# Rotary attention: the band mask is added by a matmul with the identity instead of by a VectorE addition

## The chip, the cores and the metric

The kernel runs on one core of one Trainium2 chip. The metric is device time in microseconds (us) of one execution. The kernel computes a chain of twelve transformer-like blocks; the change touches one of them, the second, and this document follows that block.

## The reference, cut to what matters

```python
x = x + _L0_attn_ref(_layernorm(x, axis=-1), Wq, Wk, Wv, Wo)   # x is (128, 32, 128)

def _L0_attn_ref(x, Wq, Wk, Wv, Wo):          # 16 query heads, 4 key/value heads of width 8
    xq = _rope((x @ Wq).reshape(b, s, HQ, HD))
    xk = _rope((x @ Wk).reshape(b, s, HKV, HD))
    xv = (x @ Wv).reshape(b, s, HKV, HD)
    keys, values = jnp.repeat(xk, N_REP, axis=2), jnp.repeat(xv, N_REP, axis=2)
    scores = jnp.einsum('bqhd,bkhd->bhqk', xq, keys) / math.sqrt(HD)
    mask = jnp.abs(idx[:, None] - idx[None, :]) <= WINDOW // 2      # WINDOW = 32
    scores = jnp.where(mask[None, None], scores, -jnp.inf)
    attn = jax.nn.softmax(scores, axis=-1)
    ctx = jnp.einsum('bhqk,bkhd->bqhd', attn, values).reshape(b, s, HQ * HD)
    return ctx @ Wo
```

A sequence has 32 positions, so a query may look at keys at most 16 positions away. The kernel puts that rule in as an addition: a constant `band`, 128 rows by 32 keys, holds 0 where a key is allowed and -1e30 where it is not.

## The kernel before

`rotary_attention` works through 32 tiles of 128 rows (four sequences of 32). A tile has a slot `s = t % 4` in every buffer and two PSUM banks of 512 f32 columns: `bank_a(s)` and `bank_b(s)`. The engines run five instruction streams, joined by semaphores only. In each stream a step `t` does work for several tiles at once, a lag behind each other; `live(k)` says that tile `t - k` exists. VectorE, ScalarE and GpSimd run their steps in a hardware loop with four tiles a pass (`pipelined`); TensorE's steps are written out one by one.

What step `t` does, in the order of each stream:

- **TensorE**: wait until VectorE has added tile t-4 to `x` (`added`), transpose tile t (L166); transpose the probabilities of t-3 (`turn`, L757); project tile t (`project`, L740 for queries and keys, L743 for values; the bank_b results are raw q, k); mix the values of t-3 (`mix`, L765); scores of t-1 (`score`, L750, four products of 128x128, `bank_b`), which signals `scored`; output product of t-3 (`out`, L774, 16 small products on 32x32 pieces of the array), which signals `out_done`. TensorE runs an f32 product as two instructions, so L750 has eight a step and L774 has 32.
- **VectorE**: rotary turn of t-1 (L699 twice, L703), signals `roped`; addition of t-4 to `x` (L186), which waits for `out_done` and signals `added`; `add_band` of t-2 (L690), which waits for `scored`, in place in PSUM; row maxima (L724); subtraction of the maxima into `prob` (L726), signals `shifted`; moments of t+2 (L119, L122); row sums and reciprocal of t-2 (L707, L709), which wait for the exponential and signal `summed`.
- **GpSimd**: normal factors of t+1; `normalise` of t-3 (L629) by the reciprocals; `mask` of t-1 (L617, L619), which spreads the turned queries and keys and signals `masked`.
- **ScalarE**: copy of the transposed tile t (L173); copy of the transposed probabilities of t-3 (L647); normalisation of t+1 (L651); exponential of t-2 (L656); copies of the mix of t-3 (L664) and of the values of t (L660).

Of the kernel before, what the change touches and what calls it, by code (L numbers as in the profile page):

```python
# [16 lines left out]
ALU = mybir.AluOpType  # L17
# [5 lines left out]
B, SEQ, D = 128, 32, 128  # L23
CTX, CD = 257, 256
P = 128
BT = P // SEQ
TILES = B * SEQ // P
HEADS = 16
# [155 lines left out]
def add_to_x(core, t, update):  # L184

    return core.nc.vector.tensor_tensor(core.x[:, ds(t, 1), :], core.x[:, ds(t, 1), :], update, ALU.add)  # L186
# [10 lines left out]
def pipelined(eng, width, first, behind, step):  # L197


    valid = lambda t: lambda lag: 0 <= t - lag < TILES  # L200
    for t in range(first, width):
        step(t, t % width, valid(t))
    with eng.Fori(1, TILES // width - 1) as it:
        for j in range(width):
            step(it * width + j, j, lambda lag: True)
    for t in range(TILES - width, TILES + behind):
        step(t, t % width, valid(t))
# [360 lines left out]
def per_row(t):  # L568

    return t.rearrange("p (r w) -> p r w", w=1).to_broadcast([P, t.shape[1], SEQ])  # L570


def rotary_attention(core, name):
# [4 lines left out]
    nc, dram = core.nc, core.dram  # L578
    W = 4
    with ExitStack() as st:  # L580
# [7 lines left out]
        q4 = sb("q4", [P, W, BT, G, SEQ])  # L588
        kbd = sb("kbd", [P, W, BT, G, SEQ])
# [8 lines left out]
        bank_b = lambda s: core.psum[:, 2 * s + 1, :]  # L598
# [7 lines left out]
        @block.sync  # L606
        def _(sp):
            load(sp, [(w_qk[:, :, :], dram[f"{name}_Wqk"]), *((w_o[32 * b:32 * b + 32, :, :], dram[f"{name}_Wo"]) for b in range(BT))], w_in)
            sp.wait_ge(zeroed, 1)
            load(sp, [(w_v[:, g, 8 * g:8 * g + 8], dram[f"{name}_Wv"][:, 8 * g:8 * g + 8]) for g in range(G)], w_in)  # L610
# [71 lines left out]
        @block.vector  # L682
        def _(dve):
            rope = core.c("rope").rearrange("p (f w) -> p f w", f=4)
            band = core.c("band").rearrange("p (a w) -> p a w", a=1).to_broadcast([P, HEADS, SEQ])

            def add_band(t, s):
                dve.wait_ge(scored, t + 1)
                raw = bank_b(s).rearrange("p (a w) -> p a w", w=SEQ)
                nc.vector.tensor_tensor(raw, raw, band, ALU.add)  # L690

            def turn_pairs(t, s):
                dve.wait_ge(projected, t + 1)
                pairs, waves = bank_b(s).rearrange("p (a f w) -> p a f w", a=2, f=2), rope.rearrange("p (a f) w -> p a f w", a=2)
                for part in range(2):
                    one = pairs[:, :, part, :].rearrange("p a (b w) -> p a b w", b=BT)
                    made = prod[:, s, :, :].rearrange("p a (b w) -> p a b w", b=BT) if part else one
                    wave = waves[:, :, part, :].rearrange("p a (b w) -> p a b w", b=1).to_broadcast([P, 2, BT, SEQ])
                    nc.vector.tensor_tensor(made, one, wave, ALU.mult)  # L699

            def join_pairs(s):
                two = bank_b(s).rearrange("p (a f w) -> p a f w", a=2, f=2)
                nc.vector.tensor_tensor(qk[:, s, :, :], two[:, :, 0, :], prod[:, s, :, :], ALU.add).then_inc(roped, 1)  # L703

            def sums(t, s):
                dve.wait_ge(exped, t + 1)
                nc.vector.tensor_reduce(total[:, s, :], prob[:, s, :, :], X, ALU.add)  # L707
                dve.drain()
                nc.vector.reciprocal(total[:, s, :], total[:, s, :]).then_inc(summed, 1)  # L709

            def step(t, j, live):
                o, q = (j - 1) % W, (j - 2) % W
                if live(1):
                    turn_pairs(t - 1, o)
                    dve.drain()
                    join_pairs(o)
                if live(4):
                    dve.wait_ge(out_done, t - 3)
                    add_to_x(core, t - 4, bank_a(j)[:, 0:D]).then_inc(added, 1)
                if live(2):  # L720
                    raw = bank_b(q).rearrange("p (a w) -> p a w", w=SEQ)
                    add_band(t - 2, q)
                    dve.drain()
                    nc.vector.tensor_reduce(top[:, q, :], raw, X, ALU.max)  # L724
                    dve.drain()
                    nc.vector.tensor_tensor(prob[:, q, :, :], raw, per_row(top[:, q, :]), ALU.subtract).then_inc(shifted, 1)  # L726
                if live(-2):
                    front.dve_moments(dve, t + 2 - (j + 2) % W, only=(j + 2) % W)
                if live(2):
                    sums(t - 2, q)  # L730

            front.dve_moments(dve, 0, only=0)
            pipelined(dve, W, -1, 4, step)

        @block.tensor
        def _(pe):
            def project(t, s):
                pe.wait_ge(front.xnT_done, t + 1)
                for f in range(4):
                    nc.tensor.matmul(bank_b(s)[:, f * P:(f + 1) * P], w_qk[:, f, :], front.xnT[:, s, :], start=True, stop=True)  # L740
                for b in range(BT):
                    for g in range(G):
                        last = nc.tensor.matmul(bank_a(s)[32 * g:32 * g + 32, b * 32:(b + 1) * 32],  # L743
                                                front.xnT[:, s, b * 32:(b + 1) * 32], w_v[:, g, :], start=True, stop=True)
                last.then_inc(projected, 1)

            def score(t, s):
                pe.wait_ge(masked, t + 1)
                for b in range(BT):
                    last = nc.tensor.matmul(bank_b(s)[:, b * P:(b + 1) * P], q4[:, s, b, :, :].rearrange("p j w -> p (j w)"),  # L750
                                            kbd[:, s, b, :, :].rearrange("p j w -> p (j w)"), start=True, stop=True)
                last.then_inc(scored, 1)

            def turn(t, s):
                pe.wait_ge(normal, t + 1)
                for b in range(BT):
                    last = nc.tensor.transpose(bank_a(s)[:, b * P:(b + 1) * P],  # L757
                                               prob[:, s, b * G:(b + 1) * G, :].rearrange("p g k -> p (g k)"), core.c("ident"))
                last.then_inc(turned, 1)

            def mix(t, s):
                pe.wait_ge(v_done, t + 1)
                pe.wait_ge(probT_done, t + 1)
                for b in range(BT):
                    last = nc.tensor.matmul(bank_b(s)[32 * b:32 * b + 32, 0:P], vbd[:, s, b, :], probT[:, s, b, :],  # L765
                                            start=True, stop=True)
                last.then_inc(mixed, 1)

            def out(t, s):
                pe.wait_ge(mixT_done, t + 1)  # L770
                for h in range(G):
                    for b in range(BT):
                        own = slice(32 * b, 32 * b + 32)
                        last = nc.tensor.matmul(bank_a(s)[own, 0:D], mixT[own, s, h, :], w_o[own, h, :], start=(h == 0),  # L774
                                                stop=(h == G - 1))
                last.then_inc(out_done, 1)

            def step(t, j, live):
                if live(0):
                    if live(4):  # L780
                        pe.wait_ge(added, t - 3)
                    front.pe_transpose(pe, t - j, only=j)
                if live(3):
                    turn(t - 3, (j - 3) % W)
                if live(0):
                    project(t, j)
                if live(3):
                    mix(t - 3, (j - 3) % W)
                if live(1):
                    score(t - 1, (j - 1) % W)  # L790
                if live(3):
                    out(t - 3, (j - 3) % W)

            pe.wait_ge(w_in, 16 * (1 + BT + G))
            for t in range(TILES + 4):
                step(t, t % W, lambda lag: 0 <= t - lag < TILES)
# [2812 lines left out]
```

## Time and profile before

| | |
|---|---|
| median of 3 runs | 3559.14 us (3554.55 to 3559.98) |
| the profiled execution's own time | 3559.38 us |
| its span in the trace | 3557.5 us |
| rotary attention in it | about 92 to 280 us |
| TensorE busy over the span | 3208.9 us (90%) |
| VectorE busy over the span | 2507.1 us (70%) |

Two kinds of view carry the argument. A table of stretches gives for each stretch of the span the busy time of each engine and, as PEclk, TensorE's granted clock as a share of full speed. A timeline gives instructions in order of time: start, duration, engine, line, operation, operands, and in brackets how long the engine had been idle before it and what released it. PE is TensorE's matmul side, PEld its weight loads, DVE VectorE, ACT ScalarE, POOL GpSimd. Matmuls overlap: of a group "x8" with duration 1.16 us, the last instruction starts about 0.27 us (one instruction's duration) before the end.

### The profile page before, as it was taken

What the parts mean: (1) busy time and instruction counts of PE and PEld (TensorE: products, weight loads), DVE (VectorE), ACT (ScalarE), POOL (GpSimd) and SP (SyncE); (2) the same over time, 40 slices, a digit from 0 to 9 for tenths busy, and PEclk for the clock granted to TensorE, in tenths of its full rate; (3) what the DMA queues carried; (4) which work ended last, traced back from release to release, by engine and by line L of the source; (5) the groups of instructions that cost most, each with busy time, mean ns of one, the idle gap of its engine ahead of it and who ended that gap; (6) DMA issues with size and microseconds to landing.
All of it is one profiled execution on the core that took longest, in us unless ns stands there. A gap on an engine that the chain in (4) does not pass through costs nothing. (4 is left out here: it accounts for less than half of the span.)

```text
span 3557.5 us, 110134 instructions
## 1 busy us (share of the span) xinstructions
PE 3208.9 (90%) x41582; PEld 2687.3 (76%) x41584; DVE 2507.1 (70%) x7190; ACT 1835.4 (52%) x4594; POOL 1260.3 (35%) x1887
## 2 busy tenths in 40 slices
PE   6886999999989999888899999999999999873866
PEld 4665999999957777546789889888998899743345
DVE  6784999999968888567455555555555555477765
ACT  4341777787768888574433333333333333343463
POOL 3673888888834343204200000000000000174042
PEclk8996999999989999998799999999999999997677
DMA  4001000000022222100465555555555555374000
GB/s 121 8 2 40 1 0 0 0 0 0 1 70 82 82 83 81 46 1 7 99 145 130 126 127 139 127 130 132 132 131 127 127 136 130 74 134 62 0 3 27
DMA packets 375654, 254.59 MB, mean 72 GB/s; under 512 B 118724, under 2 KB 371608, under 8 KB 374680
## 3 DMA queue, kind: packets, MB, share of 16 engines
q1 hardware_dynamic: 370968, 245.64, 28.4%
q10 hardware_dynamic: 4352, 4.20, 0.5%
q8 instruction: 246, 4.03, 0.5%
q14 instruction: 88, 0.72, 0.1%
HBM read 233.73 MB, written 15.75 MB: 70 GB/s over the span
## 5 line engine op out<-in xcount | busy, mean ns | idle before, releaser
L2482 PE MATMUL psum<-L_xattn_ctxT,L_xattn_q_ctx 128*128 128x257 f32 x2048 | 508.8, 389 | 2.9 <-issue 2.3
L1076 PE MATMUL psum<-L_ffn_share,L_ffn_prob 128*128 128x128 f32 x4096 | 487.9, 278 | 23.1 <-DVE L_ffn_prob L1009 15.6
L893 POOL TENSOR_TENSOR L_ffn_sums<-L_ffn_sims 128x1024 f32<-128x1024 f32 x256 | 485.4, 1913 | 61.2 <-DVE L_ffn_prob L1009 61.2
L2513 PEld LDWEIGHTS psum<-L_xattn_probT,L_xattn_ctx 32*128 32x128 f32 x16384 | 468.9, 187 | 44.5 <-issue 42.0
L1076 PEld LDWEIGHTS psum<-L_ffn_share,L_ffn_prob 128*128 128x128 f32 x4096 | 471.3, 193 | 35.8 <-DVE L_ffn_prob L1009 25.6
L2513 PE MATMUL psum<-L_xattn_probT,L_xattn_ctx 32*128 32x128 f32 x16384 | 493.2, 273 | 2.1 <-DVE L_xattn_probT L2396 2.1
L2334 ACT ACTIVATE L_xattn_prob<-psum,L_xattn_nmax 128x258 f32<-128x258 f32 x512 | 239.2, 472 | 479.9 <-DVE L_xattn_nmax L2382 463.0
L2305 POOL TENSOR_TENSOR L_xattn_z_var<-L_xattn_z_mv,L_xattn_z_eps 128x1 f32<-128x1 f32 x32 | 6.1, 192 | 1245.0 <-DVE L_xattn_z_mv L2408 1215.7
L2482 PEld LDWEIGHTS psum<-L_xattn_ctxT,L_xattn_q_ctx 128*128 128x128 f32 x2048 | 367.3, 190 | 64.8 <-issue 8.2
L935 ACT ACTIVATE psum<-L_ffn_sums,L_ffn_bias 128x512 f32<-128x512 f32 x512 | 339.1, 686 | 64.8 <-DVE L_ffn_prob L1009 60.3
L1009 DVE SCALAR_TENSOR_TENSOR L_ffn_prob<-L_ffn_sums,L_ffn_best,psum 128x512 f32<-128x512 f32 x512 | 358.1, 741 | 7.0 <-ACT psum L935 3.4
L1366 ACT ACTIVATE L_xattn_prob<-psum,L_xattn_nmax 128x289 f32<-128x289 f32 x512 | 250.0, 501 | 61.0 <-DVE L_xattn_nmax L1397 61.0
L1397 DVE TENSOR_REDUCE L_xattn_nmax<-psum 128x1 f32<-128x289 f32 x512 | 199.0, 450 | 23.0 <-PE psum L1435 22.8
L2387 DVE RECIPROCAL L_xattn_total<-L_xattn_total 128x2 f32<-128x2 f32 x256 | 41.4, 162 | 245.6 <-ACT L_xattn_prob L2334 237.4
L2328 ACT ACTIVATE L_xattn_q_heads<-psum 128x256 f32<-128x256 f32 x128 | 49.2, 384 | 317.1 <-PE psum L2454 317.1
L2396 DVE STREAM_TRANSPOSE L_xattn_probT<-L_xattn_prob 128x512 f32<-128x512 f32 x256 | 182.1, 711 | 20.5 <-issue 1.3
L2382 DVE TENSOR_REDUCE L_xattn_nmax<-psum 128x2 f32<-128x516 f32 x256 | 178.1, 696 | 18.8
L2390 DVE TENSOR_SCALAR L_xattn_prob<-L_xattn_prob,L_xattn_total 128x256 f32<-128x256 f32 x512 | 158.4, 351 | 21.3 <-issue 1.6
L2372 DVE COPY L_xattn_q_ctx<-psum 128x512 f32<-128x512 f32 x256 | 159.6, 663 | 13.5 <-PE psum L2466 13.5
L1450 PE MATMUL psum<-const,L_xattn_prob 128*128 128x128 f32 x1024 | 168.6, 288 | 0.3 <-ACT L_xattn_prob L1366 0.3
L1450 PEld LDWEIGHTS psum<-const,L_xattn_prob 128*128 128x128 f32 x1024 | 107.8, 141 | 75.4 <-issue 74.8
L2466 PE MATMUL psum<-L_xattn_q_heads,L_xattn_wk_cross 64*128 64x128 f32 x2048 | 153.4, 291 | 4.6 <-issue 2.1
(463 smaller groups left out, 6504.0 us busy)
## 6 DMA issues: line engine op xcount, KB each, us to landing
L_xattn_ctx<-ctx_dram SPq DMA_DIRECT2D x512, 256.0 KB, 3.8
L_xattn_ctxT<-ctx_T_dram SPq DMA_DIRECT2D x128, 257.0 KB, 3.3
L_xattn_k_all<-ctx_T_dram SPq DMA_DIRECT2D x128, 128.5 KB, 2.1
L_xattn_v_all<-ctx_dram SPq DMA_DIRECT2D x128, 128.0 KB, 2.2
L_attn_qkv_scratch<-L_attn_qkv SPq DMA_DIRECT2D x24, 256.0 KB, 3.2
L_attn_rows<-L_attn_qkv_scratch SPq DMA_DIRECT2D x24, 256.0 KB, 5.3
start_raw<-ctx_dram ACTq DMA_DIRECT2D x16, 256.0 KB, 11.9
L_xattn_v_rows<-L_xattn_v SPq DMA_DIRECT2D x8, 256.0 KB, 2.3
```

What stands on the lines that cost most here:

```text
L893: nc.gpsimd.tensor_tensor(sums[:, h % RING, :, :], sx, sy, ALU.add).then_inc(summed, 1)
L935: nc.scalar.activation(raw_prob(k), half(sums[:, h % RING, :, :].rearrange("p i j -> p (i j)"), k), ACT.Exp, bias=bias[:, s, h:h + 1]).the ...
L1009: nc.vector.scalar_tensor_tensor(half(prob[:, h % RING, :], k), half(sums[:, h % RING, :, :].rearrange("p i j -> p (i j)"), k), best[:, s, ...
L1076: last = nc.tensor.matmul(pair(2 * s)[:, c * P:(c + 1) * P], prob[:, h % RING, c * P:(c + 1) * P], share[:, h % RING, :], start=(h == 0 an ...
L1366: ins = nc.scalar.activation(prob[:, b % 2, g, :], scores(g), ACT.Exp, bias=nmax[:, b % 2, g:g + 1], accum_out=total[:, b % 2, g:g + 1])
L1397: nc.vector.tensor_reduce(nmax[:, b % 2, g:g + 1], scores(g), X, ALU.max, negate=True).then_inc(maxed, 1)
L1450: return [nc.tensor.transpose(turned_bank(k)[:, g, :], prob[:, b % 2, g, k * P:(k + 1) * P], core.c("ident")) for g in range(G)][-1]
L2334: ins = nc.scalar.activation(prob[:, s, g, :], scores(s)[:, g, :], ACT.Exp, bias=nmax[:, s, g:g + 1], accum_out=total[:, s, g:g + 1])
L2382: nc.vector.tensor_reduce(nmax[:, s, :], scores(s), X, ALU.max, negate=True).then_inc(maxed, 1)
L2396: nc.vector.transpose(probT[:, b % 2, :, 2 * s:2 * s + 2, :].rearrange("p k g n -> p g k n"), prob[:, s, :, 0:2 * P].rearrange("p g (k m) ...
L2482: last = nc.tensor.matmul(scores(s)[:, g, 0:CTX], q_ctx[:, p, c, b, h:h + 4, :].rearrange("p h n -> p (h n)"), ctxT[:, b, c, :], start=(c ...
L2513: last = nc.tensor.matmul(mix_bank(r)[:, c * P:(c + 1) * P], ctx[rows, b, k, c * P:(c + 1) * P], probT[rows, b % 2, k, :, :].rearrange("p ...
```

## The change

The VectorE instruction L690 and the drain behind it go; the wait for `scored` now stands straight before the row maxima. TensorE gets one product more: after `out(t-3)`, at the end of its step, it multiplies the identity (128x128) by the band, which is read with a zero step 16 times over so that it has 512 columns, and accumulates the product onto the four score blocks of tile t-1 in `bank_b`. To let it accumulate, the score products change their flags, and the signal `scored` moves from the last score product to the band product, so from before `out` to behind it. Nothing else changes: the same loads, the same constants, the same other streams.

```diff
-                    add_band(t - 2, q)
-                    dve.drain()
+                    dve.wait_ge(scored, t - 1)
                     nc.vector.tensor_reduce(top[:, q, :], raw, X, ALU.max)
...
             def score(t, s):
                 pe.wait_ge(masked, t + 1)
                 for b in range(BT):
-                    last = nc.tensor.matmul(bank_b(s)[:, b * P:(b + 1) * P], q4[:, s, b, :, :].rearrange("p j w -> p (j w)"),
-                                            kbd[:, s, b, :, :].rearrange("p j w -> p (j w)"), start=True, stop=True)
-                last.then_inc(scored, 1)
+                    nc.tensor.matmul(bank_b(s)[:, b * P:(b + 1) * P], q4[:, s, b, :, :].rearrange("p j w -> p (j w)"),
+                                     kbd[:, s, b, :, :].rearrange("p j w -> p (j w)"), start=(b == 0), stop=False)
+
+            band = core.c("band").rearrange("p (a w) -> p a w", a=1).to_broadcast([P, HEADS, SEQ])
+
+            def add_band(t, s):
+                nc.tensor.matmul(bank_b(s).rearrange("p (a w) -> p a w", w=SEQ), core.c("ident"), band, start=False,
+                                 stop=True).then_inc(scored, 1)
...
                 if live(3):
                     out(t - 3, (j - 3) % W)
+                if live(1):
+                    add_band(t - 1, (j - 1) % W)
```

The removed VectorE function was

```python
def add_band(t, s):
    dve.wait_ge(scored, t + 1)
    raw = bank_b(s).rearrange("p (a w) -> p a w", w=SEQ)
    nc.vector.tensor_tensor(raw, raw, band, ALU.add)
```

## Rows read from the trace of the kernel before

**Rows 1.** Table of stretches: the block's start and its steady part.

```profile
107.00:112.00 5.00, 3.80 (x52) 2.99 (x51) 4.11 (x9) 1.71 (x5) 2.84 (x6) 0.81 0.00 0
112.00:264.00 152.00, 132.67 (x2696) 108.11 (x2696) 133.81 (x316) 63.03 (x172) 115.03 (x169) 1.00 0.01 2
```

**Rows 2.** Timeline of all engines, steady step 17, 185.6 to 191 us.

```profile
185.67 0.28 DVE L186 TENSOR_TENSOR x_sb<-x_sb,psum 128x128 f32 x1
185.87 0.69 DVE L690 TENSOR_TENSOR psum<-psum,const 128x512 f32<-128x512 f32 x1
...
186.00 0.33 PE L166 MATMUL psum<-const,L_attn_front_xn_sb 128*128 128x128 f32 x1 [0.60 <-DVE x_sb L186]
...
186.37 0.27 ACT L173 COPY L_attn_front_xnT_sb<-psum 128x128 f32<-128x128 f32 x1 [2.48 <-PE psum L166]
186.63 0.69 DVE L724 TENSOR_REDUCE L_attn_top<-psum 128x16 f32<-128x512 f32 x1
...
186.69 1.16 PE L740 MATMUL psum<-L_attn_front_xnT_sb,L_attn_w_qk 128*128 128x128 f32 x8
...
188.05 0.45 PE L765 MATMUL psum<-L_attn_probT,L_attn_vbd 128*32 128x128 f32 x8
188.12 0.63 ACT L656 ACTIVATE L_attn_prob<-L_attn_prob 128x512 f32<-128x512 f32 x1 [0.32 <-DVE L_attn_prob L726]
...
188.43 1.16 PE L750 MATMUL psum<-L_attn_kbd,L_attn_q 128*128 128x128 f32 x8
...
188.78 0.69 DVE L707 TENSOR_REDUCE L_attn_total<-L_attn_prob 128x16 f32<-128x512 f32 x1
...
189.52 1.08 PE L774 MATMUL psum<-L_attn_w_o,L_attn_mixT 32*32 32x128 f32 x32
...
189.71 0.41 DVE L699 TENSOR_TENSOR psum<-psum,const 128x256 f32<-128x256 f32 x1
...
190.20 1.05 POOL L629 TENSOR_TENSOR L_attn_prob<-L_attn_prob,L_attn_total 128x512 f32<-128x512 f32 x1
190.52 0.42 DVE L703 TENSOR_TENSOR L_attn_qk<-psum,L_attn_prod 128x256 f32<-128x256 f32 x1
190.86 0.28 DVE L186 TENSOR_TENSOR x_sb<-x_sb,psum 128x128 f32 x1
```

**Rows 3.** Timeline of TensorE, the transpositions that open steps 4 and 18.

```profile
117.84 0.33 PE L166 MATMUL psum<-const,L_attn_front_xn_sb 128*128 128x128 f32 x1 [0.74 <-DVE x_sb L186]
...
191.19 0.33 PE L166 MATMUL psum<-const,L_attn_front_xn_sb 128*128 128x128 f32 x1 [0.60 <-DVE x_sb L186]
```

**Rows 4.** Timeline of VectorE across the end of a pass of its loop.

```profile
243.42 0.69 DVE L690 TENSOR_TENSOR psum<-psum,const 128x512 f32<-128x512 f32 x1
244.56 0.69 DVE L724 TENSOR_REDUCE L_attn_top<-psum 128x16 f32<-128x512 f32 x1 [0.44 <-issue]
```

**Rows 5.** Timeline of TensorE in another block, f32 products with 512 columns.

```profile
3443.06 1.02 PE L3245 MATMUL psum<-L_attn_soft,const 128*128 128x512 f32 x2
3443.92 1.02 PE L3246 MATMUL psum<-L_attn_soft,L_attn_diags 128*128 128x512 f32 x2
```

**Rows 6.** Timeline of all engines at the block's start, tiles 0 to 3.

```profile
107.21 0.42 PE L166 MATMUL psum<-const,L_attn_front_xn_sb 128*128 128x128 f32 x1
...
108.22 0.69 DVE L724 TENSOR_REDUCE L_attn_top<-psum 128x16 f32<-128x512 f32 x1
...
110.88 0.27 PE L166 MATMUL psum<-const,L_attn_front_xn_sb 128*128 128x128 f32 x1
...
111.19 0.27 ACT L173 COPY L_attn_front_xnT_sb<-psum 128x128 f32<-128x128 f32 x1 [0.69 <-PE psum L166]
```

**Rows 7.** Timeline of all engines at the block's end, steps 31 and 32.

```profile
259.49 0.33 PE L166 MATMUL psum<-const,L_attn_front_xn_sb 128*128 128x128 f32 x1 [0.59 <-DVE x_sb L186]
...
264.46 0.66 PE L757 MATMUL psum<-const,L_attn_prob 128*128 128x128 f32 x4 [0.39 <-POOL L_attn_prob L629]
...
265.89 0.42 PE L765 MATMUL psum<-L_attn_probT,L_attn_vbd 128*32 128x128 f32 x8 [0.77 <-ACT L_attn_probT L647]
...
269.80 0.69 DVE L724 TENSOR_REDUCE L_attn_top<-psum 128x16 f32<-128x512 f32 x1
```

More of the change, by code:

```diff
@@ L684, in _ @@
             rope = core.c("rope").rearrange("p (f w) -> p f w", f=4)
[L685 to L690, printed above, removed]
             def turn_pairs(t, s):
```

## The prediction

> **What bounds the kernel now.** I went from the coarse view to the fine one. The table of stretches for 112 to 264 us [rows 1] shows TensorE busy for 132.67 of 152 us and VectorE for 133.81: two engines almost equally full, at the full granted clock (1.00, so 2.4 GHz). A table of shares cannot say which one sets the pace, so I read one step in the timeline [rows 2]. VectorE runs from L186 at 185.67 to L186 at 190.86 without a gap that another engine ends: a step is 5.19 us of VectorE work. TensorE does wait. The transposition that opens its step stands behind "0.60 <-DVE x_sb L186" [rows 2, 3]: it waits until VectorE has added tile t-4, although the last output product of the step before began long ago. So VectorE sets the pace here, and TensorE has about 0.6 us a step to spare. The reader should see both numbers: the change takes from the first and spends from the second.
>
> The pace over the block: the transposition of step 4 begins at 117.84 [rows 3], that of step 31 at 259.49 [rows 7], 27 steps and 141.65 us, or 5.246 us a step. That is more than the 5.19 of one step, because VectorE's loop turns back after four tiles: at 244.56 the row maxima start 1.14 us after the addition before them, with 0.44 put down to issue, where the usual distance is 0.76 [rows 2, 4].
>
> **What the change takes from VectorE.** L690 and its drain go: the distance from L690 (185.87) to L724 (186.63), 0.76 us a step [rows 2]. VectorE's own step becomes 5.19 - 0.76 = 4.43. If nothing else bound, 27 steps at 0.76 would be 20.5 us. That is the gain on offer.
>
> **What it puts on TensorE.** The price of an f32 product of 128x128 weights with 512 columns has near rows: in another block L3245 also multiplies by the identity and accumulates. Its two instructions begin at 3443.06 and the next product at 3443.92 [rows 5]: 0.86 us for a product. No row shows a moving operand read with a zero step; I take the same 0.86, as the array streams the same 512 columns. From below it is bounded by two of L740's instructions, which have only 128 columns and start 0.127 apart (1.16 less 0.27, over seven gaps) [rows 2]: 0.25. From above, by twice L3245, 1.71.
>
> Now TensorE's own step without any wait, in four pieces.
> 1. From the transposition to the projection. Before it is 186.00 to 186.69, 0.69, by way of ScalarE's copy (186.37, 0.27 long) [rows 2]. When TensorE comes from work and not from a wait, the weights are already in: at 110.88 the transposition is 0.27 long and the copy starts 0.31 later, at 111.19 [rows 6]. So 0.31 + 0.27 + the 0.05 between copy and L740 = 0.63. The range of this piece is 0.63 to 0.69.
> 2. From L740 (186.69) to the last instruction of L774, which starts at 189.52 + 1.08 - 0.27 = 190.33 [rows 2]: 3.64. None of these pieces waits for another engine now, and none should later (below).
> 3. From there to the band product. Where products on quarter columns of the array (L765, last start 188.05 + 0.45 - 0.27 = 188.23) are followed by whole ones (L750, 188.43), 0.20 passes; where whole is followed by whole it is 0.127, as above [rows 2]. I take 0.20, the nearer case.
> 4. The band product, 0.86.
>
> The sum is 0.63 + 3.64 + 0.20 + 0.86 = 5.33 us, against 5.246 now. TensorE becomes the bound, and a step gets longer by 0.08, times 27 = 2.2 us. With 0.127 for piece 3 it is 5.26 and +0.3 us. The Trainium skill, TensorEngine Tiling (Array Packing), Key Properties, speaks against the change just here: changing the tiling mode drains TensorE, and L774's 32x32 pieces are such a mode. Until now the change from L774 to the transposition lay inside the idle 0.6. The rows agree with it in the 0.20 against 0.127 after L765; no row shows L774 followed at once by a whole product.
>
> **Does anything else stop TensorE?** I place the step anew from the transposition at 0. The band product's last instruction starts at -0.43 and, 0.59 long, ends at 0.16; the maxima start at 0.20. VectorE's order then runs as in [rows 2], counted from L724 at 186.63: L186 4.23 later, at 4.43. It must wait for the last L774, 0.63 + 3.64 + 0.27 = 4.54, so it starts about 4.6 and ends 4.88; 186.00 against 185.67 says that TensorE may go 0.33 after its start, 4.93. TensorE wants it at 5.33: 0.4 to spare, because `out` signals before the band product and that product covers the addition. VectorE is free for the maxima at 4.8, and they come at 5.53: 0.7 to spare, which also swallows the 0.38 of the loop's turn [rows 4]. The probabilities for L757 need L629, whose end (190.20 + 1.05) is 4.62 after L724: 4.82, before 5.33. The masks follow L703 (190.52, 3.89 after L724, so at 4.09); L750 of the next step comes at 5.33 + 0.63 + 1.74 = 7.70, 3.6 later, where now it is 3.1 (190.52 to 191.19 + 2.43) and L750 waits for nothing. The exponential (188.12) starts 1.49 after the maxima, at 1.7, when ScalarE's copies, ahead of it in its queue, are done. What loses its cover is small; the moved signal `scored` costs nothing, since the maxima of a tile come a step later anyway.
>
> **The two ends of the block.** In the start, TensorE runs partly at the lower clock: the granted clock is 0.81 over 107 to 112 [rows 1]. The first band product stands at 107.21, where the transposition is now, and takes 0.86 at the full clock and 1.71 at half. The maxima of tile 0, now at 108.22 behind L690, would start at 107.21 + 1.71 + 0.20 = 109.1, or 108.3 at full clock [rows 6]. Everything up to step 4 hangs on this tile: 0 to +0.9. I take +0.9, as the clock is still low there. At the end, step 31's transposition is at 259.49 and the maxima of the last tile at 269.80, 10.31 later [rows 7]. In the new order step 32 begins at 5.33; L765 follows 1.43 behind L757 as it does now (264.46 to 265.89, by way of ScalarE's copy) [rows 7], L750 0.38 behind, L774 1.09 behind, its last instruction 0.81 behind, then 0.20 + 0.43 + 0.59: 10.26. Nothing is won or lost, and after it the chain is the same.
>
> **Sum.** +2.2 + 0.9 - 0.05 = +3.0 us. The profiled execution took 3559.38, its span 3557.5; 3559.38 + 3.0 = 3562.4. It stood 0.24 above the median, so against the median of 3559.14 I predict 3562 us. A difference of 0.2% (7.1 us) is about what a measurement can tell from none, so this is "no change": 20.5 us taken from VectorE, 27 x (0.86 + 0.20) = 28.6 us laid on TensorE, of which its idle time hides most.
>
> **The rivals.**
> - *TensorE's step is longer than I count* (slower). The bank is accumulated, the band's weights and those of the transposition are not loaded ahead, and piece 1 stays 0.69: 0.11 more for the load and 0.06 for the piece give 5.50, so +6.9, and with +0.9 it is 3567. For it: the changed tiling shape just ahead. Against: L3245 to L3246 at 0.86 shows the next load hidden. 7%.
> - *The zero step costs* (slower, the other side). If reading the band 16 times over streams at half rate, the product is 1.71: 0.86 more on each of 32 steps, +27 us, 3589. The point at which it decides against the kernel is a product above 1.01 us (0.15 x 27 = 4.1 on top of 3.0). Nothing in the profile speaks for it; nothing rules it out. 4%.
> - *The product is cheaper than L3245*, so that the gain comes through. At half the price, 0.43, a step is 4.90: 0.35 x 27 = 9.3 us less, 3551. Against: both instructions at 0.43 in every pair of [rows 5]. 5%. By the Trainium skill (TensorE: Matmul & The Clock Gate, Back-to-back issue gap: a sustained 131 ns for a matmul of 512 columns; FP8 and Floating Point Precision, TensorE Precision Notes: four passes for true FP32) the product would be 0.52, and the time, an estimate by that page, 3553. Here the trace disagrees, with 0.86.
> - *Pieces shorter by overlap*, with TensorE at 5.20 to 5.26 and the start free: 3558 to 3560. It is no separate outcome but the low part of mine.
>
> **How the numbers follow.** My own case, TensorE bound at 5.22 to 5.40 a step, has 84%, with 3558 to 3566 as its range. The range for 8 in 10 takes the first rival's edge and the spread of the runs below: 3556 to 3567. Faster by over 0.2% needs a step under about 4.95, which only the cheaper product gives, and some chance of a cause I have not seen: 0.06. Slower by over 0.2%: the zero step's 4%, about half of the first rival's 7%, and a little for a wait that I placed wrongly: 0.10. Within: 0.84.
>
> **What would show it.** Right: TensorE's transposition no longer waits for `x_sb` L186; VectorE instead waits at L724 for the band product, about 0.5 to 0.9 us a step; the distance of transpositions is even at 5.3, without the longer fourth; two instructions with 512 columns 0.43 apart behind L774, with 0.20 between. Wrong: the two start more than 0.5 apart (second rival); L186 is still named ahead of the transposition (VectorE still bound, or its addition late); L757 or L750 waits for GpSimd.

## The result, and the profile after

| | |
|---|---|
| before, median of 5 runs beside it | 3557.28 us (3554.55 to 3559.98) |
| after, median of 5 runs | 3573.98 us (3570.66 to 3577.89) |
| ratio after / before, 95% interval | 1.0048 (1.0037 to 1.0059) |
| after, the profiled execution and its span | 3573.81 us, 3572.0 us |

The changed kernel is 16.7 us slower, 0.48%. The prediction said 3562 (3556 to 3567) and "no change": too low, and the time lies outside the range. Ratios here and below compare executions in the fast state only; a rare slow one (5327.56 us once among the eleven of e2) stays out of them.

Inside the block the picture is the one forecast. The table of stretches of the changed kernel, same steady stretch as in [rows 1]:

```profile
112.00:264.00 152.00, 152.00 (x2663) 114.93 (x2661) 114.87 (x277) 63.41 (x168) 111.52 (x164) 1.00 0.01 2
```

TensorE is busy for all of the 152 us (132.67 in [rows 1]), VectorE for 114.87 (133.81). One engine now sets the pace alone, at a granted clock of 1.00. The timeline of a steady step of the changed kernel, which answers to [rows 2] (its line numbers: band product L749, maxima L717, projection L733, scores L743, `turn` L755, `mix` L763, `out` L772):

```profile
185.58 0.27 PE L166 MATMUL psum<-const,L_attn_front_xn_sb 128*128 128x128 f32 x1
...
185.78 0.69 DVE L717 TENSOR_REDUCE L_attn_top<-psum 128x16 f32<-128x512 f32 x1 [0.62 <-PE psum L749]
...
186.21 1.16 PE L733 MATMUL psum<-L_attn_front_xnT_sb,L_attn_w_qk 128*128 128x128 f32 x8
...
189.04 1.07 PE L772 MATMUL psum<-L_attn_w_o,L_attn_mixT 32*32 32x128 f32 x32
...
190.04 1.12 PE L749 MATMUL psum<-const 128*128 128x512 f32 x2
190.29 0.29 DVE L186 TENSOR_TENSOR x_sb<-x_sb,psum 128x128 f32 x1 [0.21 <-PE psum L772]
...
191.00 0.27 PE L166 MATMUL psum<-const,L_attn_front_xn_sb 128*128 128x128 f32 x1
```

The transposition L166 carries no bracket any more: TensorE comes to it from work. The bracket has moved to VectorE's maxima, "0.62 <-PE psum L749". The addition L186 runs under the band product. And the step is 191.00 - 185.58 = 5.42 us, where 5.33 was forecast. TensorE's transpositions of steps 4 and 31 and the last maxima of the block, in the changed kernel's timeline:

```profile
115.01 0.27 PE L166 MATMUL psum<-const,L_attn_front_xn_sb 128*128 128x128 f32 x1
...
261.51 0.27 PE L166 MATMUL psum<-const,L_attn_front_xn_sb 128*128 128x128 f32 x1
...
271.97 0.69 DVE L717 TENSOR_REDUCE L_attn_top<-psum 128x16 f32<-128x512 f32 x1 [0.74 <-PE psum L749]
```

From step 4 (115.01) to step 31 (261.51) it is 146.50 us, 5.426 a step, against 141.65 and 5.246 in [rows 3, 7]: +4.85 us. For the ends one needs the block's own clock, since the loads ahead of it vary. Its first DMA issue, that of `L_attn_w_qk`, is at 92.34 before and 88.78 after. Step 4 comes 25.50 us behind it before and 26.23 after: +0.7. Step 31 to the last maxima takes 10.31 before [rows 7] and 10.46 after: +0.15. So the block costs 4.85 + 0.7 + 0.15 = +5.7 us, and the distance from its first DMA issue to that of the next block says the same: 187.27 before, 193.00 after.

That leaves about 11 us of the 16.7, and they are not in the block that was changed. Cutting both traces at the first weight load of every block shows them. Early in wide attention, for one, the longest block (1366 us), TensorE's timeline of the changed kernel has

```profile
1799.70 3.80 PE L2482 MATMUL psum<-L_xattn_ctxT,L_xattn_q_ctx 128*128 128x257 f32 x8 [4.25 <-DMA L_xattn_ctx<-ctx_dram]
```

where the kernel before has at the same tile

```profile
1790.47 2.00 PE L2482 MATMUL psum<-L_xattn_ctxT,L_xattn_q_ctx 128*128 128x257 f32 x8 [0.54 <-DMA L_xattn_ctx<-ctx_dram]
```

This code is the same in both, instruction by instruction. The wait is 3.7 us longer, and the eight products behind it take 3.80 us instead of 2.00, because the granted clock has fallen meanwhile, to 0.50; in the kernel before it is 1.00 from 1791 to 1796 us. Table of stretches, changed kernel:

```profile
1799.00:1804.00 5.00, 4.30 (x12) 3.57 (x13) 0.40 (x2) 0.00 (x0) 0.00 (x0) 0.50 1.07 181
```

Why unchanged blocks take longer is what most of the experiments ask.

### The profile page after: what moved, and what is told of

The parts are those of the page before. It is cut to its first block and busy times, and to the rows that moved or that the text cites. A ratio compares the mean times of both kernels' runs of the same rounds, so it can differ in the third digit from the quotient of the medians.

```text
span 3572.0 us, 110198 instructions
## 1 busy us (share of the span) xinstructions
PE 3236.1 (91%) x41646; PEld 2694.8 (75%) x41648; DVE 2491.0 (70%) x7158; ACT 1837.9 (51%) x4594; POOL 1260.5 (35%) x1887
## 5 line engine op out<-in xcount | busy, mean ns | idle before, releaser
L2372 DVE COPY L_xattn_q_ctx<-psum 128x512 f32<-128x512 f32 x256 | 159.7, 663 | 11.7 <-PE psum L2466 11.6
```

## The experiments

Theories. **A (block):** TensorE's longer step makes all of it; what is seen elsewhere is scatter. **B (place of the code):** the change makes VectorE's program 24 instructions shorter (the addition and the drain in 12 written-out steps, 6137 to 6113) and TensorE's 32 products longer (128 in the trace, where an f32 product is two loads and two matmuls). All code behind it moves, and loops and streams behind run slower for it. Block lengths below are distances between first weight loads in the one profile of each kernel; the totals are medians of 4 to 12 runs. The recorded expectations use other names: in those of e1 and e2 "Theory A" is the moved code and "Rival C" chance; in those of e3 and e4 "A1" is TensorE's moved code and "B" VectorE's.

### Repeats: e1, e2

The changed kernel and the kernel before, unedited, on another chip.

> The changed kernel, unchanged, for a second profile. In the first profile the rotary block itself was 5.7 us longer than before (from its first instruction to its last addition), the start of the program 3.6 us shorter and everything behind the block 12.3 us longer, though no line of it was changed. Theory A (the rest is slower because the added and removed instructions move the code of the later loops): the time is 14 to 18 us above before again, and the same places lose the same: +0.12 us on every second tile in the product-key block, some us at the start of the wide attention. Rival C (the rest is chance of single profiles, by transfers): the places and sizes differ from the first profile, and the total comes closer to +6.

> The kernel before, unchanged, for a second profile: how far do two profiles of one program differ, block by block? Theory A: under 1 us in the blocks behind the rotary one, so that a +12 there cannot be chance; the time within 0.1% of before. Rival C: several us from profile to profile, in the blocks that move much data.

Measured: after again 3577.45 us (3573.05 to 3581.11), ratio 1.0054 (1.0040 to 1.0068); before again 3557.41, ratio 1.0000 (0.9991 to 1.0009). The loss is real. The step in e1 is 5.43 again. Against e2's profile the second profile of the changed kernel is longer by 5.6 us in rotary attention, 2.7 in the product-key block, 3.3 in context attention, 2.2 in the gated scan and 5.3 in wide attention, while the two profiles of the kernel before differ by at most 0.3 in all of these but the first (1.1). The two profiles of the changed kernel agree less well: up to 1.7 us apart in one of these blocks. Most of the gated scan's 2.2 can be seen. Its table of stretches in e1, with TensorE's timeline:

```profile
1528.00:1531.00 3.00, 1.83 (x8) 0.82 (x6) 2.92 (x4) 2.27 (x5) 0.00 (x0) 1.00 0.00 0
1531.00:1533.00 2.00, 1.10 (x2) 0.63 (x3) 1.84 (x9) 1.94 (x3) 0.00 (x0) 0.82 0.00 0
1533.00:1535.00 2.00, 2.00 (x3) 0.67 (x2) 0.47 (x5) 1.99 (x2) 1.21 (x2) 0.50 0.00 0
...
1531.90 8.49 PE L1809 MATMUL psum<-L_attn_xnT,L_attn_w_u 128*128 128x512 f32 x16 [2.07 <-DVE L_attn_ub L1745]
```

and in e2 the same place of the program, which there comes 14.5 us earlier in the span:

```profile
1518.50:1520.50 2.00, 2.00 (x6) 0.92 (x6) 0.46 (x5) 1.99 (x2) 1.21 (x2) 1.00 0.03 8
...
1517.40 6.79 PE L1809 MATMUL psum<-L_attn_xnT,L_attn_w_u 128*128 128x512 f32 x16 [2.07 <-DVE L_attn_ub L1745]
```

In both TensorE is busy for 2.93 of 5 us and has the same idle stretch of 2.07 us. In e1 the granted clock then falls to 0.50, the lower of its two levels (1.2 GHz of 2.4), and the 16 products take 8.49 us; in e2 it stays at 1.00 and they take 6.79. So 1.7 of the 2.2 us are the clock, and the idle stretch alone doesn't explain its fall; these rows don't show what does. The first profile of the changed kernel has the same 8.49.

### VectorE's code put back: e3

```diff
                     raw = bank_b(q).rearrange("p (a w) -> p a w", w=SEQ)
+                    dve.drain()
+                    dve.drain()
                     dve.wait_ge(scored, t - 1)
```

> The changed kernel with two drains in VectorE's step ahead of its wait for the scores, where the addition and its drain have gone, so that VectorE's stream has as many instructions as before and its later code lies where it lay. The wait has 0.6 us to spare, so the block itself should not change (step 5.42). Theory B (VectorE's moved code costs what is lost behind the block): the product-key block loses its +0.12 on every second tile, and of the 12 us most go: 3562 to 3565. Theory A1 (TensorE's 128 added instructions cost it): no change, 3572 to 3576.

Measured: 3568.71 us (3563.97 to 3572.61), ratio 1.0035 (1.0021 to 1.0048). The step is 5.427, the block's +5.6 us is that of e1 to a hundredth. The drains lie in VectorE's wait and do nothing, and yet 8.7 us of the 19 above e1's "before" are gone. In the profile the product-key block is at +0.9 us instead of +2.7, context attention at +0.1 instead of +3.3, the gated scan at -0.1 instead of +2.2. Theory A falls: a part of the loss goes with the length of VectorE's code and not with its work. The forecast of 3562 to 3565 was still too low by 4 us, so VectorE's code isn't all of it.

### TensorE's code moved in the kernel before: e4, e5

```diff
         def _(pe):
+            for k in range(32):
+                nc.tensor.matmul(core.psum[0:1, 7, k:k + 1], core.c("ident")[:, 0:1], core.c("ident")[:, 0:1], start=True, stop=True)
             pe.wait_ge(filled, 1)
```

They stand at the start of the block behind rotary attention, where TensorE idles; e5 has 64.

> The kernel before, with 32 one-column products of one number on TensorE at the start of the block behind rotary attention, where TensorE waits 5.9 us: as many TensorE instructions as the band products, so that TensorE's later code lies where it lies in the changed kernel; the rotary block is untouched. Theory A1 (TensorE's moved code): +10 to +12, 3567 to 3570. Theory B (VectorE's moved code): within 2 us of before, 3557 to 3559. Rival C: within 2 us.

> The kernel before with 64 instead of 32 of the tiny products on TensorE behind rotary attention: 256 instructions instead of 128. If what costs is where TensorE's later code lies against blocks of 256 instructions in which it is fetched (as the Trainium skill has it in Runtime: NRT & Kernel Launch, Instruction fetch mechanics), a shift by a whole block costs nothing again: 3556 to 3560, wide attention within 1 us of before, and TensorE's wait for the context at its start back from 4 us to under 1. If what costs is the mere number of instructions, or their being there, it is at least as slow as with 32: 3562 or more.

Measured: 32 products, 3562.11 us, ratio 1.0012 (1.0003 to 1.0021); 64 products, 3559.32, ratio 1.0005 (0.9996 to 1.0015). The shift that the change makes to TensorE's code costs the kernel before about 4 us, between what the two theories said. Twice the shift, 256 instructions of the trace, costs no more than once, so it isn't the extra work. Whether it costs less is not settled: the intervals overlap, and e5's profile (3564.83, the slowest of its eleven) lacks the sign that was forecast, wide attention back to within 1 us and its wait under 1 us. Wide attention is 6.6 us longer than in e2, the wait 3.5 us.

### What the order and the form of the band product are worth: e6, e7, e8

e6 is e3 with the band product ahead of `out`, so that no change of the array's tiling stands ahead of it, but nothing covers the addition either:

```diff
+                if live(1):
+                    add_band(t - 1, (j - 1) % W)
                 if live(3):
                     out(t - 3, (j - 3) % W)
-                if live(1):
-                    add_band(t - 1, (j - 1) % W)
```

> The changed kernel (with VectorE's two drains a step) with the band product straight behind the scores, ahead of the output product. Theory (the band product behind the output product hides VectorE's addition of tile t-4): now the transposition must wait again for that addition, which starts when the output product is done. Step: 0.63 + 3.64 + 0.86 for the band, less 0.05 to 0.1 because no weight load is exposed there, plus 0.27 + 0.05 + 0.33 from the last output product to the transposition, 5.7 to 5.8 us instead of 5.42, so about +9 us: 3577 to 3579. Rival (the two orders cost the same, since the same products run): 3568 to 3570.

Measured: 3578.52 us (3577.54 to 3586.94), ratio 1.0061 (1.0045 to 1.0077). The timeline of TensorE and its weight loads in e6:

```profile
187.57 0.30 PEld L751 LDWEIGHTS psum<-const 128*128 128x128 f32 x2
187.68 1.02 PE L751 MATMUL psum<-const 128*128 128x512 f32 x2
188.63 1.08 PE L774 MATMUL psum<-L_attn_w_o,L_attn_mixT 32*32 32x128 f32 x32
190.24 0.33 PE L166 MATMUL psum<-const,L_attn_front_xn_sb 128*128 128x128 f32 x1 [0.53 <-DVE x_sb L186]
```

Behind whole-array products the band product is 1.02 for two, as L3245 [rows 5], not 1.12: its weight load, at 187.57, begins ahead of the product and under the one before. But the transposition waits for L186 again, and a step is 5.97 us, more than the 5.7 to 5.8 expected. From the last `out` instruction (188.63 + 1.08 - 0.27 = 189.44) to the transposition it is 0.80. The place behind `out` is right: the 0.5 us that it hides are worth more than the 0.1 that it costs, and e6 is 9 to 10 us slower than e3. That its time fell into the forecast is partly luck. In its profile (3586.94, the slowest of four) the block is 16.9 us longer than in e3, which would put e6 7 us higher, though the later code lies alike in both. Either its block is often shorter than in that one execution, or less is lost behind it; no run tells which.

e7 keeps the order and makes the product cheap. The band holds only 0 and -1e30 and the identity 0 and 1, so bfloat16 copies serve (the -1e30 is rounded, and is as good a mask); they take one instruction instead of two:

```diff
+        ident_h, band_h = sb("ident_h", [P, P], BF16), sb("band_h", [P, SEQ], BF16)
...
+            nc.vector.tensor_copy(ident_h[:, :], core.c("ident")).then_inc(w_in, 1)
+            nc.vector.tensor_copy(band_h[:, :], core.c("band")).then_inc(w_in, 1)
...
-                nc.tensor.matmul(bank_b(s).rearrange("p (a w) -> p a w", w=SEQ), core.c("ident"), band, start=False,
+                nc.tensor.matmul(bank_b(s).rearrange("p (a w) -> p a w", w=SEQ), ident_h[:, :], band, start=False,
```

It also has the two drains of e3, so that VectorE's code keeps its length.

> The changed kernel with the identity and the band in bf16 (two copies on VectorE at the block's start; 0 and 1 are exact, -1e30 is rounded), which is one pass and one instruction instead of two of two, and with VectorE's stream as long as before. Theory (TensorE's own step bounds the block and the band's length is on it): the band product is 0.21 instead of 0.86, the step 5.42 - 0.64 = 4.78 against 5.25 before, so 27 x 0.47 = 12.7 us less than before in the block, less 1 to 2 at its start. TensorE's later code moves by 64 instructions, which may give 0 to 5 back: 3546 to 3553. Rival (VectorE or the chain of waits bounds at 5.0 or more once the product is short): under 7 us gained in the block.

> As the bf16 band, with 48 tiny products behind the block, so that TensorE's later code is moved by exactly 256 instructions. If blocks of 256 instructions are what matters, the blocks behind cost what they cost before, and the gain of the block is all there: 3545 to 3548. Otherwise as the bf16 band or slower.

Measured: e7 3550.73 us (3548.39 to 3555.95), ratio 0.9984 (0.9975 to 0.9993), faster than both kernels; e8, with 48 tiny TensorE products behind the block, 3552.24, ratio 0.9989 (0.9980 to 0.9998), no better. TensorE's timeline in e7:

```profile
183.03 0.33 PE L166 MATMUL psum<-const,L_attn_front_xn_sb 128*128 128x128 f32 x1 [0.20 <-DVE x_sb L186]
...
186.54 1.07 PE L778 MATMUL psum<-L_attn_w_o,L_attn_mixT 32*32 32x128 f32 x32
187.55 0.39 PE L755 MATMUL psum<-L_attn_band_h,L_attn_ident_h 128*128 128x512 bf16 x1
188.14 0.33 PE L166 MATMUL psum<-const,L_attn_front_xn_sb 128*128 128x128 f32 x1 [0.20 <-DVE x_sb L186]
```

One instruction instead of two, and the step is 5.11 us, not the 4.78 that TensorE's work alone would allow: the addition is the bound again, now by its latency, as the rival of the expectation said (5.0 or more). The block is 6.5 us shorter than in e2, not 12.7. The last `out` instruction starts at 187.34, the transposition at 188.14, the same 0.80 as in e6, and 188.14 - 183.03 = 5.11 is that chain. The band product fits into it and is free. e8's forecast, 3545 to 3548 if a shift by 256 costs nothing, failed.

### VectorE's code moved elsewhere: e9 to e12

e9 puts 24 drains outside the block into the changed kernel, at a wait of VectorE in the next block's start; e10 puts the same into the kernel before; e11 gives the kernel before 232 drains at three such waits (232 = 256 - 24); e12 is e7 without its drains (22 instructions fewer than e7).

```diff
             ins.then_inc(cov_w_done, 1)
+            for _ in range(24):
+                dve.drain()
             dve.wait_ge(stats_made, 1)
```

> The changed kernel with 24 drains on VectorE behind the rotary block, where VectorE waits 8 us for TensorE anyway: VectorE's code behind that point lies where it lay before the change, and the rotary block itself is the changed one without any drain. Theory (the place of VectorE's code costs the 8.7 us that the drains inside the step gave back): 3565 to 3569, that is +8 to +11 against before. Rival (the drains inside the step helped by what they do there): as the changed kernel, +16 to +19.

> The kernel before with 24 drains on VectorE behind the rotary block, so VectorE's later code moved by 24 instructions the other way. Theory (its place matters): something between 0 and +8 us, that this theory alone can't tell; rival (the 8.7 us have nothing to do with the place of VectorE's code): within 1.5 us of before.

> The kernel before with 232 drains on VectorE behind the rotary block, in three places where it waits 4 to 8 us for TensorE. 232 forward is 24 back, to a multiple of 256. If VectorE's code costs by its place in blocks of 256 instructions, this is the changed kernel's VectorE in the kernel before: +7 to +10 us, with 1.5 to 3 us in each of context attention and the gated scan, as in the changed kernel's profile. Rival: the drains show only where they stand, 0 to +3.

> The bf16 band without the drains, so VectorE's stream is 22 instructions shorter than before. Block itself as with the drains or 0.1 us a step shorter: 6 to 7 us less than before. Theory (place of VectorE's code): 8 us are lost behind the block, 3557 to 3560, no gain. Rival: 3549 to 3552.

Measured, each against the kernel before on its own chip: e9 3568.57 us, 1.0025 (1.0015 to 1.0036), so the drains needn't be in the block to give back what e3 gave back. e10 3562.74, 1.0011 (1.0002 to 1.0020): the same drains make the kernel before slower, so they are no good in themselves. In its profile 3.9 of the 7.1 us lost outside the rotary block are in the gated scan, with the fall of the clock seen in e1. e11 3562.22, 1.0011 (1.0002 to 1.0020): a loss, but half of what was expected; context attention is longer as forecast (+2.7), the gated scan is not (-0.3). e12 3560.14, 1.0003 (0.9995 to 1.0012): without the drains the whole gain of e7 is gone: 0.0019 of ratio, some 7 us, for 22 instructions that do nothing.

### Both put back, and TensorE's alone: e13, e14

e13 is the changed kernel with e9's 24 drains and e4's 32 tiny products (TensorE's later code then lies 256 instructions of the trace further than before). e14 has the products only.

> The changed kernel with 24 drains on VectorE and 32 tiny products on TensorE behind the rotary block, so that behind it VectorE's code lies where it lay and TensorE's is moved by 256 instructions, a whole block. Theory (the change costs 5 us in its own block, and the rest by where the later code of the two engines lies): what is left is the block, +4 to +7 against before. Rival (something else of the change costs outside its block): as with VectorE's code alone put back, +9 to +10, or more.

> The changed kernel with only TensorE's later code moved to a whole 256 instructions, VectorE's left 24 earlier. Theory: between the changed kernel and the one with VectorE's code put back: the block's 5 us and VectorE's 8 to 9, +13 to +15 against before, with the 2 to 3 us in context attention still there. Rival (TensorE's place costs nothing in the changed kernel): as the changed kernel, +17 to +19.

Measured: e13 3564.45 us (3559.68 to 3570.73), 1.0023 (1.0013 to 1.0034); e14 3568.09 (3565.52 to 3570.44), 1.0030 (1.0018 to 1.0043). Both forecasts were missed: e13 is 0 to 1 us above its +4 to +7, e14 is 2 us below its +13 to +15. The lengths of blocks, in us against e2, with every block but rotary attention and the first load summed in the last column:

| profile | VectorE code | TensorE code | rotary | context attention | gated scan | wide attention | all other than rotary |
|---|---|---|---|---|---|---|---|
| before | 0 | 0 | +1.1 | 0.0 | 0.0 | -0.2 | -0.5 |
| after | -24 | +128 | +6.8 | +1.9 | +1.7 | +6.2 | +11.7 |
| e1 (after) | -24 | +128 | +5.6 | +3.3 | +2.2 | +5.3 | +15.5 |
| e3 | 0 | +128 | +5.6 | +0.1 | -0.1 | +3.3 | +4.4 |
| e9 | 0 behind | +128 | +7.0 | -0.1 | -0.1 | +6.0 | +7.1 |
| e14 | -24 | +256 | +5.6 | +1.4 | +0.2 | +2.4 | +9.6 |
| e13 | 0 behind | +256 | +5.7 | -0.1 | -0.1 | +2.1 | +0.6 |
| e6 | 0 | +128 | +22.5 | 0.0 | 0.0 | +6.1 | +6.9 |
| e4 (before) | 0 | +128 | +1.1 | -0.9 | 0.0 | +5.7 | +4.7 |
| e5 (before) | 0 | +256 | +0.2 | 0.0 | -0.1 | +6.6 | +6.4 |
| e10 (before) | +24 | 0 | +0.3 | -0.3 | +3.9 | +2.4 | +7.1 |
| e11 (before) | +232 | 0 | +1.6 | +2.7 | -0.3 | +6.7 | +16.2 |
| e7 | 0 | +64 | -6.5 | -1.5 | +3.6 | +2.1 | +2.7 |
| e8 | 0 | +256 | -5.4 | -1.5 | +3.9 | +1.9 | +4.8 |
| e12 | -22 | +64 | -4.9 | +2.7 | +0.3 | +4.4 | +9.3 |

Three things can be read. Context attention is longer, by 1.4 to 3.3 us, in the five profiles in which VectorE's code behind the block lies 22 to 24 instructions earlier or 232 later, and in none of the others (there -1.5 to +0.1). The gated scan goes another way: it is longer, by 1.7 to 3.9 us, in the profiles of after, e1, e7, e8 and e10, the five in which the granted clock falls to 0.50 some 50 us into it, and these have VectorE's code at -24, 0 and +24. So what the drains seemed to give back there in e3 can't be put down to the code's place alone. And with both engines' code put back (e13) what is left in the profile is the block, +5.7 and +0.6. But one profile is one execution: e13's was the second fastest of its nine runs (3560.10, median 3564.45) and e3's its fastest (3563.97), e9's the slowest of eight (3573.11), so the column does not settle the last few us. Nor does the profile's span settle more in general: the load ahead of the first block alone varies by 5 us (-0.6 to +4.6 against e2) among the profiles.

By the ratios: after +0.48 and +0.54%, VectorE put back +0.25 and +0.35%, TensorE put back +0.30%, both +0.23%. The block's 5 to 5.7 us are 0.15%. The code's place makes 0.25 to 0.3%, 9 to 11 us, and the two engines' shares don't add: either one put back takes most of it away. The Trainium skill (Runtime: NRT & Kernel Launch, Instruction fetch mechanics) says that instructions come in blocks of 256 fetched in sequence, and that a taken branch out of the fetched window stalls. The runs agree in part: -24 and +232 have the same effect on context attention. TensorE's +256 costs less than +128 in the changed kernel (e14, 1.0030 against 1.0048 and 1.0054), not clearly less in the kernel before (e5), and brings nothing beside e9 (e13) or beside e7's +64 (e8). No row here shows a fetch, e11's total was half of what that rule led me to expect, and e10's +24 also costs. So: that 22 to 24 idle instructions of VectorE change the time of unchanged blocks is shown, and that it is their place and not what they do where they stand follows from e3 and e9, which give back about the same from two places. That it is by fetching is argued.

## Why the prediction was wrong

**Right, by the profile after.** TensorE became the bound, its transposition lost the wait for L186, the even distance replaced the longer fourth, VectorE waits at the maxima (0.62 for 0.7 forecast), L186 runs under the band product. Piece 1 was 0.63 (185.58 to 186.21), as forecast; piece 2, 3.64 (186.21 to the last `out` start, 189.04 + 1.07 - 0.27 = 189.84: 3.63); piece 3, 0.20 (to 190.04). The zero step costs nothing: in e6 the product takes as long as L3245. The gain on offer, 20.5 us, did go to nothing: 1.16 us a step (0.96 + 0.20) came onto TensorE. Its other work takes 5.42 - 1.16 = 4.26 us, so of the old step of 5.246 it had only 0.98 to spare.

**A mis-sized term: piece 4, the band product, 0.86.** It is 0.96 (190.04 to 191.00), the first of its two instructions taking 0.53. e6 shows the cause by its absence: behind whole-array products the pair is 1.02 long, behind `out`'s 32x32 pieces 1.12. The band's weights aren't loaded ahead across the change of tiling. In e6 their load starts 0.11 us before the product; in the changed kernel it starts with the product, 0.20 behind the last start of `out`:

```profile
190.04 0.30 PEld L749 LDWEIGHTS psum<-const 128*128 128x128 f32 x2 [0.20 <-issue]
```

This is the load that my first rival named (at 0.11) and that I gave 7%. The row was there. In [rows 2] L750's eight take 1.16 behind the same kind of change, and I divided this by seven gaps and called 0.127 the plain pitch; with 0.11 as the pitch, the first gap is 0.1 longer. 0.10 x 27 = 2.6 us. The start cost +0.7 for +0.9 (the first band product did run mostly at the lower clock: 1.69 us for its pair, at a mean of 0.61), the end +0.15 for -0.05. With these the block's sum is +5.7 where I had +3.0, and the time would have been 3565, inside the range and still "no change".

One more size was off, without harm here. The prediction lets the transposition go 0.66 us after the last start of `out` (4.93 less 0.63 and 3.64); in e6 and e7 it takes 0.80. So the step can't be shorter than about 5.1 us in this order, as e7 shows, and the rival of the cheaper product, with 4.90 and 3551 us, was worked out without that bound.

**The step that failed: the sum itself.** "+2.2 + 0.9 - 0.05 = +3.0" runs over one block and is added to the whole span, which puts the other eleven blocks at nothing, without a reason. They took about 11 us longer, four fifths of the 13.7 by which the measured +16.7 exceeds +3.0. No rival had it, though the change visibly shortens VectorE's code and lengthens TensorE's. The runs that show it are e3 and e9 (same step, 7 to 10 us less), e4 and e10 (kernel before, its blocks unchanged, about +4 us each) and e7 against e12 (some 7 us for 22 idle instructions).

**What stays open.** Why with both put back the median is still 2 to 3 us above what the block explains; why wide attention is about 2 to 7 us longer in every profile but the two of the unedited kernel before, mostly with a longer wait for a DMA at its start and a lower clock behind it, but in e8 and e10 (+1.9 and +2.4) without either, and there with a clock of 0.50 for 3.4 us near its end; why the clock falls in the gated scan of five profiles behind an idle stretch that e2 has too; and the mechanism. A cost that depends on distance from a boundary of the code and one that depends on a hit-or-miss meeting of transfers in wide attention would both fit what was run.

## What to carry to other kernels

In a kernel with several blocks in one program, a small edit moves all code behind it, and that alone made 0.1 to 0.3% here: before believing a result of that size, time the same edit with the code's length put back (drains in a wait, tiny products in an idle stretch), and the old kernel with the length changed. A product behind a change of the array's tiling starts later (0.20 us behind the last start instead of 0.11) and also pays its first weight load (0.10); read such prices from a group's first gap, not from its mean. And a mask of 0 and -1e30 needs no f32: as one bf16 product hidden in the latency of `out`, addition and transposition, the same idea gives 3550.7 us, 0.16% faster than before.

## What the runs showed of the hardware that was not expected

- The length of code that does nothing matters: 22 to 24 VectorE instructions, 7 to 10 us of 3557 in the changed kernels (e1 against e3, e7 against e12), about +4 us in the kernel before (e10).
- Context attention, a block with unchanged code, is 1.4 to 3.3 us longer at two placements of VectorE's code 256 instructions apart, and at none of the others tried.
- TensorE's granted clock fell from 1.00 to 0.50 in the gated scan of e1 behind an idle stretch of 2.07 us that e2 has too, without the fall; 16 products took 8.49 us instead of 6.79. The same fall stands in the profiles of after, e7, e8 and e10.
- In wide attention of the changed kernel a wait of 4.25 us for a DMA was followed by a granted clock of 0.50: eight products took 3.80 us, against 2.00 in the kernel before.
- A moving operand with a zero step, one row of 32 read 16 times over, streams as fast as a plain one: 1.02 us for two instructions of 512 columns, equal to L3245's.
